# One order of steps for all engines becomes an order of its own for each engine

## The reference

```python
x = x + tanh(g_xattn[0]) * L0_xattn(_layernorm(x), ctx)   # top-32 attention of 4 heads over 77 keys gives FiLM
                                                          # scales; S4D long convolution by FFT; FFN; layernorm
x = x + tanh(g_ffn[0])   * L0_ffn(_layernorm(x))          # butterfly matrices up, gelu, down
x = x + tanh(g_xattn[1]) * L1_xattn(_layernorm(x), ctx)   # softmax attention of 16 heads
x = x + tanh(g_ffn[1])   * L1_ffn(_layernorm(x))          # mixture of 8 experts, the best 2 per token
```

## Time and profile before

| | us |
|---|---|
| time, median of 3 runs | 411.92 (411.9 to 414.21) |
| time of the profiled execution | 411.81 |
| its span | 410.0 |
| TensorE, VectorE, ScalarE, POOL busy | 312.0, 279.1, 214.1, 106.5 |

### The profile page before, as it was taken

How to read it: one execution, slowest core, us unless ns; L and a number is a source line. 1 busy time by engine, 2 the same in 40 slices (tenths; PEclk the granted TensorE clock), 3 DMA queues, 4 the chain that set the end, 5 groups by cost and what they waited for, 6 DMA issues and landing times.

```text
span 410.0 us, 5286 instructions
## 1 busy us (share of the span) xinstructions
PE 312.0 (76%) x1518; PEld 156.5 (38%) x1518; DVE 279.1 (68%) x1219; ACT 214.1 (52%) x438; POOL 106.5 (26%) x172
## 2 busy tenths in 40 slices
PE   3310018097655899999989898979999999979895
PEld 1100015083342467745645333535444345223341
DVE  4997299998999889989587982482324457150353
ACT  4999505521305550399533468444777825717352
POOL 0599701216412846730340130040000000000000
PEclk9855558666959698899999999998999999678987
DMA  8910000000000000000000000000000000000001
GB/s 269 409 72 0 0 2 2 2 2 0 0 1 1 1 2 1 0 2 1 0 0 2 2 1 2 1 0 2 0 2 0 1 27 0 2 0 2 26 0 51
DMA packets 2625, 9.05 MB, mean 22 GB/s; under 512 B 548, under 2 KB 549, under 8 KB 2341
## 3 DMA queue, kind: packets, MB, share of 16 engines
q1 hardware_dynamic: 2596, 8.72, 5.6%
HBM read 7.67 MB, written 1.05 MB: 21 GB/s over the span
## 4 chain that ended last, share of the span: by engine, by line
PE 45%; DVE 14%; ACT 6%; issue 3%; DVEq 0%
PE bank L415 44%; DVE MT L957 3%; DVE R L1054 3%; ACT L731 2%; DVE V L1047 2%; DVE arena L957 2%; ACT arena L734 2%; ACT RS L734 1%; ACT pack_bfly L734 1%; DVE LO L957 1%; DVE XG L957 1%; DVE sel L987 0%; DVE pack_bfly L957 0%; DVE sm L991 0%; ACT E L734 0%
## 5 line engine op out<-in xcount | busy, mean ns | idle before, releaser
L731 ACT ACT_TABLE_LOAD x30 | 38.5, 1283 | 49.7 <-PE bank L415 24.0
L734 ACT ACTIVATE arena<-bank 128x512 f32<-128x512 f32 (+3 forms) x75 | 38.2, 569 | 17.7 <-PE bank L415 16.9
L734 ACT ACTIVATE E<-bank,negm 128x77 f32<-128x77 f32 x64 | 15.5, 326 | 55.6 <-DVE negm L961 55.6
L1054 DVE MATCH_REPLACE8 R<-V,R 128x77 f32<-128x77 f32 x192 | 40.5, 222 | 0.0
L1020 DVE TENSOR_REDUCE pack_bfly<-bank 128x4 f32<-128x308 f32 x64 | 26.0, 469 | 19.6 <-PE bank L415 19.6
L415 PE MATMUL bank<-arena 128*32 128x16 f32 (+3 forms) x304 | 12.7, 215 | 34.7 <-DVE arena L957 34.7
L1331 POOL TENSOR_TENSOR k0bd<-sel,w 128x308 f32<-128x308 f32 x16 | 11.3, 709 | 86.3 <-DVE w L961 86.1
L1047 DVE MAX8 V<-R 128x8 f32<-128x77 f32 x192 | 31.2, 224 | 0.0
L415 PE MATMUL bank<-pack_dft,arena 128*128 128x256 f32 x64 | 20.0, 482 | 12.8 <-DVE arena L957 12.8
L415 PE MATMUL bank<-arena,pack_dft 128*128 128x256 f32 (+1 forms) x96 | 29.3, 455 | 0.2 <-issue 0.2
L415 PE MATMUL bank<-LO,pack_first 128*128 128x512 f32 x48 | 26.1, 640 | 2.8 <-ACT LO L734 2.8
(11 more groups left out here) (202 smaller groups left out, 698.4 us busy)
## 6 DMA issues: line engine op xcount, KB each, us to landing
pack_bfly<-in_bfly SPq DMA_DIRECT2D x1, 2420.0 KB, 10.8
pack_dft<-in_dft SPq DMA_DIRECT2D x1, 1536.0 KB, 14.2
X<-in_x SPq DMA_DIRECT2D x4, 256.0 KB, 12.9
out_x<-X SPq DMA_DIRECT2D x4, 256.0 KB, 2.0
pack_ffn<-in_ffn SPq DMA_DIRECT2D x1, 512.0 KB, 14.9
pack_first<-in_first SPq DMA_DIRECT2D x1, 474.0 KB, 4.5
pack_moe<-in_moe SPq DMA_DIRECT2D x1, 452.0 KB, 15.6
pack_att<-in_att SPq DMA_DIRECT2D x1, 413.0 KB, 15.2
```

The costliest lines, as they stand in the source:

```text
L731: nc.scalar.add_instruction(mybir.InstLoadActFuncSet(name=nc.get_next_instruction_name(), act_func_set_id=need, ins=[], outs=[]))
L734: return nc.scalar.activation(out, in_, func, **kw)
L1054: nc.vector.match_replace(R8[:, g % 2, r % 2, h, :], V8[:, g % 2, h, r, :], src, NEG)\
```

## The change

ORDER becomes four lists, for TensorE, ScalarE, VectorE and POOL, and each engine's loop goes over its own. The lists hold the same steps as before; a name that has no part on the engine emits nothing there. TensorE's list also sets the PSUM banks. The counters of the layer norms are numbered by the list of the engine that signals: CENTERED and SUMMED by TensorE's, SQUARED and VARS by ScalarE's. A few waits are added where one common order had been enough before. No operation is added or removed; ScalarE's table loads become 28 instead of 30 by the order of its functions. The later parts of the lists and the lines that only exchange SCHEDULE for `SCHEDULE["act"]`, `["dve"]`, `["pool"]` are left out.

```diff
-ORDER = """
-s_consts s_kgen0 s_masks s_k0 center0/0 s_cols s_kgen1 s_vw s_ufly var0/0 s_m0 s_kgen2 weigh0/0 score0/0 s_kgen3
-s_kgen4 s_kgen5 s_kern0 score1/0 center0/1 vw/0 s_kern1 weigh1/0 score2/0 var0/1 s_kern2 weigh2/0 s_kern3 score3/0
-s_w1 s_freq weigh3/0 s_udense score0/1 vw/1 weigh0/1 attnT/0 film_in/0 score1/1 xt/0 film_pre/0 mix/0 center0/2
-dft/0 weigh1/1 score2/1 idft/0 film_out/0 score3/1 center1/0 weigh2/1 vw/2 weigh3/1 var0/2 s_misc var1/0 s_t1
-score0/2 s_dfly attnT/1 ffn_up0/0 ffn_up1/0 film_in/1 film_pre/1 xt/1 center2/0 score1/2 ffn_down/0 dft/1 mix/1
-score2/2 s_wup vw/3 s_bup var2/0 weigh0/2 idft/1 s_dhigh x1/0 center0/3 weigh1/2 film_out/1 s_dlow score3/2
-center3/0 weigh2/2 s_t2 center1/1 var3/0 var1/1 weigh3/2 var0/3 fold_up0/0 ffn_up0/1 score0/3 ffn_up1/1 attnT/2
-fold_up1/0 s_wdn score1/3 ffn_down/1 fold_down/0 film_in/2 k1/0 center2/1 center4/0 xt/2 var2/1 var4/0 dft/2
-weigh0/3 x1/1 s_v1 q/0 mix/2 center3/1 weigh1/3 film_pre/2 scoreA0/0 var3/1 idft/2 film_out/2 scoreA1/0 fold_up0/1
-scoreA2/0 fold_up1/1 score2/3 center1/2 fold_down/1 var1/2 score3/3 k1/1 ffn_up0/2 weigh2/3 scoreA3/0 center4/1
...
-"""
-SCHEDULE = [(step, int(b or 0)) for step, _, b in (word.partition("/") for word in ORDER.split())]
-CENTERS = [x for x in SCHEDULE if x[0].startswith("center")]
-MADE = [x for x in CENTERS if x[0] != "center2"]
-VARS = [x for x in SCHEDULE if x[0].startswith("var")]
+ORDER = {
+    "pe": """
+        s_k0 x1/0 s_kgen0 mix/0 center0/0 var0/0 mix/1 weigh0/0 s_vw vw/0 center2/0 center0/1 s_m0 weigh1/0 score0/0
+        score1/0 weigh2/0 score2/0 score3/0 s_dfly var0/1 s_w1 s_kern0 vw/1 attnT/0 weigh3/0 s_kern1 s_masks s_kern2
+        s_kern3 film_in/0 weigh0/1 s_ufly weigh1/1 film_pre/0 s_t1 score0/1 s_kgen1 score1/1 center0/2 weigh2/1 xt/0
+        s_freq dft/0 s_wup weigh3/1 score2/1 score3/1 center0/3 var0/2 s_bup idft/0 weigh0/2 center1/0 score0/2
+        var1/0 weigh1/2 weigh2/2 attnT/1 film_in/1 mix/2 film_pre/1 xt/1 score1/2 film_out/0 dft/1 ffn_up0/0
+        ffn_up1/0 score2/2 ffn_down/0 s_t2 var2/0 idft/1 film_out/1 score3/2 s_wdn s_kgen2 center1/1 var1/1 vw/2
+        s_cols center3/0 var0/3 var3/0 s_kgen3 s_consts k1/0 s_misc weigh3/2 ffn_up0/1 ffn_up1/1 score0/3 fold_up0/0
+        fold_up1/0 center2/1 attnT/2 fold_down/0 film_in/2 score1/3 ffn_down/1 center4/0 xt/2 var2/1 s_kgen4 var4/0
+        dft/2 center3/1 q/0 vw/3 k1/1 var3/1 scoreA0/0 film_pre/2 score2/3 fold_up0/1 fold_up1/1 idft/2 film_out/2
+        fold_down/1 scoreA1/0 center1/2 scoreA2/0 center4/1 var1/2 s_v1 scoreA3/0 var4/1 ffn_up0/2 score3/3
+        ffn_up1/2 maxT/0 ffn_down/2 keyA0/0 s_dlow weigh0/3 weigh1/3 keyA1/0 mixA0/0 keyA2/0 attnT/3 mixA1/0
+        center2/2 film_in/3 mixA2/0 xt/3 var2/2 dft/3 normA/0 wo/0 k1/2 center3/2 center5/0 k1/3 q/1 var5/0
...
+    "act": """
+        s_kgen0 center0/0 var0/0 s_vw s_kgen1 vw/0 s_m0 center0/1 s_cols s_kgen2 score0/0 score1/0 s_kgen3 score2/0
+        score3/0 s_kgen4 var0/1 vw/1 attnT/0 s_kern1 s_kern3 film_pre/0 score0/1 s_t1 center0/2 xt/0 s_freq score1/1
+        dft/0 s_wup score2/1 var0/2 score3/1 center1/0 var1/0 score0/2 attnT/1 film_pre/1 xt/1 score1/2 dft/1
+        ffn_up0/0 ffn_up1/0 center2/0 score2/2 s_t2 var2/0 s_wdn center1/1 center0/3 var1/1 vw/2 center3/0 score3/2
...
+    "dve": """
+        s_consts s_kgen0 s_kgen1 var0/0 s_k0 s_masks s_kgen2 s_cols score0/0 score1/0 score2/0 score3/0 s_kgen3
+        weigh3/0 s_kgen4 s_kgen5 s_w1 var0/1 s_kern1 s_kern3 film_in/0 film_pre/0 score0/1 score1/1 mix/0 score2/1
+        film_out/0 score3/1 var0/2 weigh3/1 s_bup score0/2 film_in/1 film_pre/1 var1/0 score1/2 mix/1 score2/2
+        var2/0 film_out/1 x1/0 score3/2 var1/1 var0/3 var3/0 s_misc weigh3/2 score0/3 film_in/2 fold_down/0 score1/3
+        var2/1 x1/1 var4/0 mix/2 var3/1 scoreA0/0 film_pre/2 score2/3 film_out/2 fold_down/1 scoreA1/0 scoreA2/0
+        s_v1 var1/2 scoreA3/0 maxT/0 var4/1 score3/3 weigh3/3 film_in/3 normA/0 var2/2 x1/2 wo/0 mix/3 var5/0
+        film_pre/3 scoreA0/1 var3/2 film_out/3 scoreA1/1 scoreA2/1 scoreA3/1 units0/0 maxT/1 var1/3 fold_down/2
...
+    "pool": """
+        s_kgen2 s_ufly weigh0/0 var0/0 weigh1/0 weigh2/0 weigh3/0 s_udense s_dfly mix/0 s_dlow weigh0/1 var0/1
+        weigh1/1 weigh2/1 weigh3/1 s_dhigh mix/1 weigh0/2 var0/2 weigh1/2 s_v1 weigh2/2 k1/0 weigh3/2 var0/3
+        weigh0/3 k1/1 mix/2 weigh1/3 weigh2/3 weigh3/3 mix/3 k1/2 k1/3
+    """,
+}
+
+SCHEDULE = {engine: [(step, int(b or 0)) for step, _, b in (word.partition("/") for word in words.split())]
+            for engine, words in ORDER.items()}
+CENTERED = [x for x in SCHEDULE["pe"] if x[0].startswith("center") and x[0] != "center2"]
+SQUARED = [x for x in SCHEDULE["act"] if x[0].startswith("center")]
+SUMMED = [x for x in SCHEDULE["pe"] if x[0].startswith("var")]
+VARS = [x for x in SCHEDULE["act"] if x[0].startswith("var")]
 
 
...
-    for at, (step, b) in enumerate(SCHEDULE):
+    for step, b in SCHEDULE["pe"]:
...
-                pe.wait_ge(squared, CENTERS.index((f"center{i}", b)) + 1)
+                pe.wait_ge(squared, SQUARED.index((f"center{i}", b)) + 1)
...
-                    act.wait_ge(centered, MADE.index((step, b)) + 1)
+                    act.wait_ge(centered, CENTERED.index((step, b)) + 1)
...
-                    act.wait_ge(variance, VARS.index((step, b)) + 1)
+                    act.wait_ge(variance, SUMMED.index((step, b)) + 1)
...
                 elif step == "xt":
                     act.wait_ge(s["xt_ready"], b + 1)
+                    if b == 0:
+                        act.wait_ge(s["qc_done"], 1)
...
                 elif step == "dft":
+                    if b == 0:
+                        act.wait_ge(s["kern_ready"], 4)
...
                 elif step == "film_pre":
                     act.wait_ge(s["film_out_ready"], 2 * b + 1)
                     if b == 0:
+                        act.wait_ge(s["qc_done"], 1)
...
                 elif step == "s_wup":
                     act.wait_ge(s["wup_ready"], 1)
+                    act.wait_ge(s["freq_ready"], 2)
...
                 elif step == "s_wdn":
                     act.wait_ge(s["wdn_ready"], 1)
+                    act.wait_ge(s["freq_ready"], 2)
```

More of the change, by code:

```diff
@@ L427, in var @@
             def var(i, b):
-                pe.wait_ge(squared, CENTERS.index((f"center{i}", b)) + 1)
+                pe.wait_ge(squared, SQUARED.index((f"center{i}", b)) + 1)
                 mm(claim(f"var{i}", b)[:, :], J, SQ[:, b, :]).then_inc(variance, 1)
             XT2 = XG
-            for step, b in SCHEDULE:
+            for step, b in SCHEDULE["pe"]:
                 tile = int(step[-1]) if step[-1].isdigit() else 0
@@ L741, in settle @@
                 act.wait_ge(s["act_link"], link[0] - back)
-            for step, b in SCHEDULE:
+            for step, b in SCHEDULE["act"]:
                 tile = int(step[-1]) if step[-1].isdigit() else 0
@@ L997, in weigh @@
                     ts(w4[:, g % 2, :], sm[:, 1, :], tm4[:, g:g + 1], None, ALU.mult).then_inc(s["weights_ready"], 1)
-            for step, b in SCHEDULE:
+            for step, b in SCHEDULE["dve"]:
                 tile = int(step[-1]) if step[-1].isdigit() else 0
@@ L1370, in dense_high @@
                 return last
-            for step, b in SCHEDULE:
+            for step, b in SCHEDULE["pool"]:
                 tile = int(step[-1]) if step[-1].isdigit() else 0
```

27 lines of the change are left out of this document (26 added, 1 removed).

## The result

| | before | after |
|---|---|---|
| time, median | 411.91 us (410.84 to 414.21) | 379.55 us (378.72 to 379.86) |
| span of the profiled execution | 410.0 | 377.6 |
| TensorE busy + gaps, whole span | 312.0 + 98.0 | 301.9 + 75.7 |
| busy + gaps up to `score0/2` | 55.0 + 79.4 | 60.6 + 64.4 |
| busy + gaps from there to the end | 257.0 + 18.6 | 241.25 + 11.35 |

The kernel is faster: 0.9204 of the time before, 95% interval 0.9163 to 0.9246. A second measurement of the changed kernel gave 378.58 (378.43 to 378.64). Of 32.4 us of span the forecast had 17.6.

What follows compares the result with a forecast made beforehand. VectorE was taken to lead up to 134.4 us, TensorE after. `score0/2` at 126.3, plus 249.6 busy, 2.5 new and 18.6 old gaps, less 4.6, gave 392.4 of span; plus 1.8, 394 us, range 384 to 407.

Steps and rivals of the forecast that it cites:

- Step 1: VectorE up to `mix/0`: the 10.9 us stall goes, 2.8 of new waits come; `mix/0` at 101.1, 8.1 earlier.
- Step 2: From `mix/0` to TensorE's `score0/2`, with `s_wup` and `s_bup` moved ahead: `score0/2` at 126.3 against 134.40, 8.1 us earlier.
- Step 3: TensorE from `score0/2` on: 249.6 us busy, 2.5 of new gaps, 18.6 of old gaps less 4.6; span 392.4.
- (a): Gaps go nearly everywhere; behind `score0/2` only the last 4.8 us and 2.5 remain: 385 us; chance 0.15.
- (b): POOL keeps its slow pace in `s_ufly` (21.2 us), VectorE stalls 6.3, no later gap saved: 405 us; chance 0.15.
- (c): After 126 TensorE waits for whole top-k tiles, 6.8 us each at up to four places: 421 us, slower; chance 0.06.
- (d): Score tiles ahead of `s_kgen3` only delay `s_kern0` by 13.7 us: 407 us up to no change; chance 0.09.

Runs made afterwards that it cites:

- the run with POOL's new head alone: Kernel before with only `s_kgen2` moved to the front of POOL's list, ahead of `s_ufly` and `var0/0`: 404.09 us.
- the run that moves them back: Changed kernel with `s_wup`, `s_bup`, `s_dhigh` back behind `score2/2` and `center0/3` back behind `idft/1`: 387.89 us.
- the join: Changed kernel's lists regrouped: steps up to the old `moe_out/0` first, then the others, each in their new order: 383.61 us.
- The run with the old end: Changed kernel's lists up to the old `moe_out/0`, the old common order for the steps behind it: 388.36 us.
- the common order: Changed kernel with TensorE's new list, some steps put later, as one order for all four engines: 439.01 us.
- the two moves: Changed kernel with `maxT/2` behind `top2/1` on VectorE and `top2/1` ahead of `maxT/2` on ScalarE: 383.62 us.

## Why the prediction was right or wrong

**Step 1, right, with errors that cancel.** `mix/0` was put at 101.1 and began at 101.65; `s_kern0` at 73.2, began at 74.72. The stall of VectorE is gone. The rule that `mix/0` moves by idle time alone was not exact: VectorE's busy time ahead of it rose by 1.7 (90.10 to 91.78), and the wait of `s_cols` was 3.43, not 2.2; against these, the three small waits of before (1.03, 0.45, 0.55) are gone, which the forecast had kept. POOL's first seven products took 10.11, not 3.2. That costs nothing (POOL waited for the ratio anyway and was done at 30.7; 31.1 forecast). The Trainium skill, "SBUF — State Buffer", SBUF: two separate sides, calls the port pair of the two engines an exclusive lock. The runs fit it: the seven products take 10.11 beside VectorE's passes of `s_kgen1` (7.15 to 17.1) and 3.42 in the run with POOL's new head alone, at the same place (8.44), where these passes begin only at 13.55.

**Step 2, right to 1.3 us, in part by luck.** `idft/0` 109.47 (111.8 forecast), 6.19 long (5.0 forecast), `score0/2` 125.0 (126.3). The early start of `idft/0` and its length offset each other; in the second profile, with 3.70, `score0/2` stood at 123.6. The moved steps were put at 9.5, less 1.0 for the later `score0/2` in the run that moves them back, which lost 8.3.

**Step 3, wrong.** This is where the forecast failed. It put 249.6 of busy time and 16.5 of gaps behind `score0/2`; there were 241.25 and 11.35. The miss is 8.35 + 5.15 = 13.5 us, with step 2's 1.3 the whole 14.8.

- The failing sentence is "The others I keep, since the list after `moe_out/1` is nearly the same". I judged the lists by TensorE's alone, from a point too late, and took 2.06 and 2.57 off. The order from around `moe_out/0` on is worth 8.8 us of time, 9.1 of span (4.1 around the join, 4.7 behind it), and five pairs on ScalarE and VectorE, which TensorE's list doesn't show, carry 5.9 to 6.6.
- The busy time was taken as fixed. I wrote that the forecast falls with a clock lower than that of before, and didn't ask what a higher one would give: 0.93 to 0.97 over 250 us. The price of a gap is the gap and the slow products behind it. The run with the old end shows both terms: 3.8 of gaps bring 5.3 of busy time with them.
- 13.5 less 9.1 leaves 4.4 us, 3.1 busy and 1.3 gaps, in the middle (125 to 310). No run has that part alone. Its size is borne out: with the old beginning, all later lists give 395.09 and the last ones alone 406.54; of these 11.5 us 4.1 are the join, and 7.4 are left for the middle (6 to 13 by the spread of the first run), against the 4.4 and the 4.6 that the forecast had, 9.0. Which steps of it carry the 4.4 stays open.

**The rivals.** (a), gaps gone nearly everywhere, 385, was nearest and still 5.5 too high: the gaps were 4.1 more than it had, and the busy time 8.35 less. (b) POOL's pace: its butterfly products took 1.5 us a stage beside top-k tiles, as hoped. (c) didn't happen in the changed kernel (its longest wait for ASUM or XG after 126 is 0.91); the common order shows its mechanism (8.99). (d) didn't happen: the work behind `s_kern0` shrank.

## What to carry to other kernels

A list per engine lets an engine do a short piece while it would wait for something else; look for the places where the engine that doesn't lead stands idle ahead of a step of which only a later part is needed by the leader. When gaps of TensorE go, its busy time goes down too, so count a gap at more than its length, here at 1.2 (the two moves) to 2.5 times (the join: 1.7 us of gaps and 2.5 of busy time). Halves of a schedule need not add up: here 7 and some 16 us alone made 32 together, and early work may be of use only if the steps that fill the time come with it. Read all engines' lists, and from the first step that moves, before calling a part unchanged.
